# Two later attentions of a transformer chain on one core: the bound on the squared norms is taken by GpSimd, right in front of its power, and the sums of squares alternate between two places

## The reference

```python
def l2norm(t):
    return t / jnp.clip(jnp.linalg.norm(t, axis=-1, keepdims=True), 1e-12)
...
h = shift_token(x)
qkv = h @ wqkv
q, k, v = jnp.split(qkv, 3, axis=-1)
q, k, v = (to_heads(q), to_heads(k), to_heads(v))
q = l2norm(q) * qs
k = l2norm(k) * ksc
q, k = rotary_xpos(q, k)
o = local_attention(q, k, v)      # windows of 128, each with the one before
x = x + o @ wo
```

## Time and profile before

| | before |
|---|---|
| median of 3 runs | 1781.7 us (1779.3 to 1782.6) |
| the profiled execution | 1780.4 us, its span 1778.7 |
| TensorE matmuls busy | 1709.4 us, 96% of the span |
| VectorE busy | 1544.5 us, 87% |
| ScalarE busy | 1164.5 us, 65% |
| GpSimd busy | 1046.2 us, 59% |
| TensorE's granted clock, whole span | 0.993 |

### The profile page before, as it was taken

One profiled execution on the slowest core, in us unless ns is written; L12 is line 12 of the kernel. 1 busy time (PEld: TensorE's weight loads), 2 busy tenths in 40 slices (PEclk: granted clock), 3 DMA queues, 4 the chain that ended last, 5 costly groups with the idle time before them and its releaser, 6 DMA issues.

```text
span 1778.7 us, 43290 instructions
## 1 busy us (share of the span) xinstructions
PE 1709.4 (96%) x15168; PEld 1464.3 (82%) x15168; DVE 1544.5 (87%) x3863; ACT 1164.5 (65%) x3024; POOL 1046.2 (59%) x996
## 2 busy tenths in 40 slices
PE   6999999999999899999998999989999999999997
PEld 4787777789998788888887888868888888878886
DVE  7888888868878899999997677789999999967776
ACT  6999988854445687877775434357777777743332
POOL 3676566534434677777673455367778777634343
PEclk9999999999999999999999999999999999999999
DMA  3111211032322222222223434332222222141221
GB/s 107 38 38 38 72 40 32 26 107 79 108 69 76 84 65 80 62 78 77 64 68 95 144 105 127 100 105 72 71 69 77 65 78 73 50 117 54 82 83 36
DMA packets 183075, 133.83 MB, mean 75 GB/s; under 512 B 21080, under 2 KB 182112, under 8 KB 182112
## 3 DMA queue, kind: packets, MB, share of 16 engines
q1 hardware_dynamic: 182880, 131.37, 24.4%
HBM read 92.52 MB, written 38.80 MB: 74 GB/s over the span
## 4 chain that ended last, share of the span: by engine, by line
PE 63%; DVE 13%; ACT 13%; issue 7%; DMA 2%; SPq 1%; POOL 0%; DVEq 0%; ACTq 0%; POOLq 0%
PE psum L601 14%; PE psum L603 14%; PE psum L602 14%; ACT b_probs L1864 5%; PE psum L716 3%; PE psum L698 3%; PE psum L937 3%; DVE masked L1361 3%; PE psum L905 3%; PE psum L918 2%; ACT a_probs L1745 2%; PE psum L879 2%; PE psum L651 1%; DVE a_neg_max L1229 1%; DVE psum L1227 1%
## 5 line engine op out<-in xcount | busy, mean ns | idle before, releaser
L1864 ACT ACTIVATE b_probs<-masked,neg_max 128x256 f32<-128x256 f32 (+1 forms) x512 | 249.9, 490 | 133.1 <-DVE neg_max L1361 133.1
L601 PE MATMUL psum<-wa_hi,b_h_hi 128*128 128x512 f32 (+1 forms) x576 | 234.7, 407 | 5.0 <-DVE wa_lo L1156 3.4
L603 PE MATMUL psum<-wa_hi,b_h_lo 128*128 128x512 f32 (+1 forms) x576 | 215.8, 375 | 0.0
L602 PE MATMUL psum<-wa_lo,b_h_hi 128*128 128x512 f32 (+1 forms) x576 | 214.9, 373 | 0.0
L601 PE MATMUL psum<-g_h_hi,wm_hi 128*128 128x512 f32 (+1 forms) x480 | 190.8, 397 | 3.5 <-POOL g_h_lo L2129 2.4
L2089 POOL TENSOR_TENSOR g_in<-g_in,minus_half 128x16 f32<-128x16 f32 x64 | 187.8, 2935 | 4.5 <-DVE g_in L1313 4.5
L603 PE MATMUL psum<-g_h_hi,wm_lo 128*128 128x512 f32 (+1 forms) x480 | 189.4, 395 | 0.0
L602 PE MATMUL psum<-g_h_lo,wm_hi 128*128 128x512 f32 (+1 forms) x480 | 189.2, 394 | 0.0
L1361 DVE CUSTOM_DVE_ANT_0 masked<-psum,mask 128x256 f32<-128x256 f32 (+1 forms) x512 | 176.6, 407 | 7.1 <-PE psum L905 7.0
L1483 POOL TENSOR_TENSOR g_in<-g_z,g_in 128x512 f32<-128x512 f32 x62 | 80.3, 1296 | 162.8 <-DVE g_in L1307 157.7
L601 PE MATMUL psum<-wm_hi,u_hi 128*128 128x256 f32 x576 | 164.0, 285 | 0.1
(11 more groups left out here) (168 smaller groups left out, 5533.7 us busy)
## 6 DMA issues: line engine op xcount, KB each, us to landing
b_inv_t<-inverse_rows SPq DMA_DIRECT2D x128, 128.0 KB, 3.1
x_mid<-y_out SPq DMA_DIRECT2D x96, 128.0 KB, 2.3
rope_in<-in_rope SPq DMA_DIRECT2D x64, 128.0 KB, 2.3
x_res<-x_state SPq DMA_DIRECT2D x64, 128.0 KB, 2.8
g_in<-x_mid SPq DMA_DIRECT2D x32, 256.0 KB, 3.8
g_old<-x_state SPq DMA_DIRECT2D x16, 512.0 KB, 4.1
out_x<-g_fin SPq DMA_DIRECT2D x15, 512.0 KB, 2.9
w_raw<-in_w_mlp_b SPq DMA_DIRECT2D x2, 2154.0 KB, 8.8
```

The source lines that it names most:

```text
L601: nc.tensor.matmul(out, a_hi, b_hi, start=first, stop=False)
L602: nc.tensor.matmul(out, a_hi, b_lo, start=False, stop=False)
L603: return nc.tensor.matmul(out, a_lo, b_hi, start=False, stop=last)
L1864: ins = nc.scalar.activation(out, src, ACT.Exp, bias=neg_max[:, r, k:k + 1], scale=-1.0, accum_out=row_sum[:, n % 2, 4 * r + k:4 * r + k + 1])
```

## The change

GpSimd now takes the maximum with 1e-24 itself, as a new instruction directly in front of its power, with the constant in the instruction; VectorE's L1313 and the tile `least` are gone. The sums of squares go to one of two places by the parity of the block, and VectorE waits before it writes a place until the power of two blocks ago is done. `rotate_q` gets a wait for VectorE's own sums, which read the squares that it overwrites.

```diff
--- before.py
+++ after.py
@@ -186,7 +186,6 @@
         ident = sbuf("ident", [P, P])
         zero_row = sbuf("zero_row", [P, 2, P])
         minus_half = sbuf("minus_half", [P, 16])
-        least = sbuf("least", [P, 16])
         b_inv = sbuf("b_inv", [P, 32])
         b_inv_turned = sbuf("b_inv_turned", [P, 32])
         vec_a = sbuf("vec_a", [P, 16])
@@ -245,7 +244,8 @@
         g_in_flat = [t[:].rearrange("p c a d -> p (c a d)") for t in g_in]
         cos_part = [g_in_flat[0][:, 512 * i:512 * i + 512] for i in range(2)]
         rope = g_in_flat[0][:, 1024:1280].rearrange("p (a d) -> p a d", a=4)
-        norm2, norm2c, rnorm = [g_in_flat[0][:, 1280 + 16 * i:1296 + 16 * i] for i in range(3)]
+        norm2 = [g_in_flat[0][:, 1280 + 16 * i:1296 + 16 * i] for i in range(2)]
+        norm2c, rnorm = [g_in_flat[0][:, 1312 + 16 * i:1328 + 16 * i] for i in range(2)]
         rot = [g_in_flat[1][:, 512 * i:512 * i + 512] for i in range(2)]
         b_ctx.close()
 
@@ -1304,16 +1304,14 @@
             def norms(n, i):
 
                 v.wait_ge(S[["q_squared", "k_squared"][i]], g0 + n + 1)
-                nc.vector.tensor_reduce(norm2[:, 8 * i:8 * i + 8], heads(squares[i][:, n % 2, :]), AX.X,
+                if g0 + n > 1:
+                    v.wait_ge(S["rnorm_ready"], g0 + n - 1)
+                nc.vector.tensor_reduce(norm2[n % 2][:, 8 * i:8 * i + 8], heads(squares[i][:, n % 2, :]), AX.X,
                                         ALU.add).then_inc(S["norm2_part"], 1)
-                if i == 0:
-                    v.wait_ge(S["norm2_part"], 2 * (g0 + n) + 2)
-                    if g0 + n > 0:
-                        v.wait_ge(S["rnorm_ready"], g0 + n)
-                    nc.vector.tensor_tensor(norm2c[:], norm2[:], least[:], ALU.max).then_inc(S["norm2_ready"], 1)
 
             def rotate_q(n):
                 v.wait_ge(S["rope_ready"], g0 + n + 1)
+                v.wait_ge(S["norm2_part"], 2 * (g0 + n) + 2)
                 rotate(nc.vector, 0, n, S["q_parts"])
                 v.wait_ge(S["q_parts"], 4 * (g0 + n) + 3)
                 nc.vector.tensor_tensor(cos_part[0][:], cos_part[0][:], squares[0][:, n % 2, :], ALU.add).then_inc(S["q_parts"], 1)
@@ -1670,7 +1668,6 @@
         def _(v):
             nc.vector.memset(zero_row[:], 0.0)
             nc.vector.memset(big[:], -MASKED)
-            nc.vector.memset(least[:], 1e-24)
             nc.vector.memset(b_inv[:], 1.0)
             nc.vector.memset(minus_half[:], -0.5).then_inc(consts_set, 1)
             dve_attention_a(v)
@@ -2085,6 +2082,8 @@
             def inverse_norms(n):
                 if g0 + n > 0:
                     pool.wait_ge(S["k_rot"], g0 + n)
+                pool.wait_ge(S["norm2_part"], 2 * (g0 + n) + 2)
+                nc.gpsimd.tensor_scalar_max(norm2c[:], norm2[n % 2][:], 1e-24).then_inc(S["norm2_ready"], 1)
                 pool.wait_ge(S["norm2_ready"], g0 + n + 1)
                 nc.gpsimd.tensor_tensor(rnorm[:], norm2c[:], minus_half[:], ALU.pow).then_inc(S["rnorm_ready"], 1)
```

## The result

The changed kernel takes 1787.7 us (median of 6 executions, 1785.5 to 1789.2), the kernel before beside it 1780.9 (1779.3 to 1782.6): 1.0036 times as long, 95% interval 1.0026 to 1.0047. Taken again later, beside other executions of before, it was 1787.3, 1.0036 [1.0023, 1.0049]. Forecast were 1778.3 and a range up to 1783.5, so it is slower where I had a small gain, and outside the range. The profiled execution took 1786.4 us, its span 1784.7.

What follows compares the result with a forecast made beforehand. The chain through VectorE's maxima and ScalarE's exponentials was taken to set the pace, TensorE right behind. Plain steps -5.7, split steps +2.8, opening -0.5 gave -3.4 us: 1778.3 for the median, range 1772.5 to 1783.5.

Steps and rivals of the forecast that it cites:

- Plain steps: Later two attentions, steps without a weight split on GpSimd: 12.35 us each, 0.15 shorter, 38 x 0.15 = 5.7 us saved.
- Rival 2: Another wait, on ScalarE or TensorE, takes the max's place at once in plain steps; 1783.2 us at most; chance 0.17.
- Split steps: Steps with GpSimd's weight split ahead of the power: 14 x 0.20 = 2.8 us lost; S is a step's scores' start (L905).
- d: Delay of GpSimd's power by the new maximum and its self-wait: 0.24 us, with ends 0.15 and 1.24.
- rival 3: GpSimd's max is dear, delaying the power before L2072 and L1336: 1783.9 us, or 1798 with a 1.16 start; chance 0.11.
- The two that "escape": Two of 16 split steps, behind a block's short first step where the power has more room, counted as losing nothing.
- The opening: Second layer's opening: L1566, directly behind L1313, can come sooner; 0.5 us saved, bounds 0 and 0.7; first layer 0.
- The memset less: One memset fewer in the changed kernel, counted as worth nothing.

Runs made afterwards that it cites:

- before again: The kernel before, unchanged, run and profiled a second and a third time: 1781.4 us (12 executions) and 1779.5 us (one).

## Why the prediction was wrong

**Plain steps: right.** Forecast -0.15 x 38, measured -0.19 x 38 = -7.2 (36 of them among the 27 steps of each layer, -6.8), the upper bound that I gave; a little of it comes from the addresses. The idle time in front of the maxima is 0.60 us, not 0.8. Rival 2 is out: nothing else took the place of the wait.

**Split steps: here it failed.** I wrote that "a split step grows by d - 0.04 = 0.20 us", with the power ending at S + 6.89 and the tables starting at S + 6.85. The power ended at S + 7.32, they start at S + 7.30, and the step grew by 0.61. The size of d was off too (0.33 to 0.35 for my 0.24), but that would have given 0.30, inside the range. What failed is that I let the power keep its length: the hold added 0.28 us to it, and the 14 split steps cost 8.5 us where I had 2.8. I had read the mutual hold of VectorE and GpSimd as something that befalls VectorE, because L1313 shows it that way nearly 64 times; whichever is issued second waits. The rows were there. The rotation at 759.53 stood 0.20 us behind the power at 759.33, while my own two terms moved the rotation forward by 0.19 and the power back by 0.24. And the trace of before has three powers that are held, two of them at the openings, by the very rotation in question; GpSimd and VectorE:

```profile
550.88 3.29 POOL L2089 TENSOR_TENSOR g_in<-g_in,minus_half 128x16 f32<-128x16 f32 x1 [4.36 <-DVE g_in L1313]
```
```profile
550.73 0.68 DVE L1483 TENSOR_TENSOR g_in<-g_h,g_in 128x512 f32<-128x512 f32 x1
```

From the crossing on, while the power starts inside the rotation's first instruction, its end hangs on that instruction's end and no longer on d. So rival 3, whose price was d x 14, had the right place and the wrong mechanism: my forecast of it turned slower only from a maximum of 0.67 us, and 0.26 did it. None of the three signs that I had named for being wrong came up (plain steps above 12.3 us, split steps shorter, a maximum over 0.4 us), since none of them looked at the power.

**The two that "escape": wrong.** They did not: the short first step grew by 0.3 and the one behind it by 0.9 to 1.1 in each layer, +2.6 together. In the short first step of before the power starts at S + 2.44 and the rotation at S + 2.89; in after the rotation comes first, at S + 2.62, and the power at S + 2.80 takes 3.30 us. GpSimd so enters the next step 0.46 us later than before (its first low half at S + 1.22 instead of S + 0.76), and there the room of 0.45 us that the power had ahead of the rotation is gone. In the second layer it is the maximum that is held in this step, 0.74 us long, and the power behind it keeps its 2.93.

**The opening: right, with a neighbour left out.** Forecast -0.5 for the second layer, measured -0.67 (from the mark at 1147 us to the first step's start, in both profiles of after; 0.0 in the two of before again). The first step of each layer lost another 0.57, which I had not counted. L1313 stood there between the sum of squares and the low halves of the keys (L1340), for which TensorE waits before the next scores; VectorE in before:

```profile
577.50 0.53 DVE L1313 TENSOR_TENSOR g_in<-g_in,least 128x16 f32<-128x16 f32 x1
577.95 0.68 DVE L1340 TENSOR_TENSOR k_t_lo<-psum,k_t_hi 128x512 fp32r<-128x512 f32 x1
```

The low halves start at S + 12.10 there and at S + 11.54 in after, and the next step comes as much sooner.

**What I had left out: the addresses.** "The memset less: nothing" is as forecast, but the tile less moved all that lies behind it by 64 bytes. That cost 2.1 to 2.8 us in the first attention and the first MLP, 1.9 of them in the MLP.

By the runs' numbers the sum is -6.8 (36 plain steps) + 8.5 (14 split) + 2.6 (the two, with the short ones) - 0.8 (the ends) - 1.1 (the first steps) - 0.7 (the opening) + 2.5 (addresses) = +4.2. Measured are +6.2: 1787.5, the median of the 12 executions of after, less 1781.3, that of 84 of before. Some 0.4 of the other 2.0 are in the second layer's second step; where the rest is stays open. The start and each layer's second step vary by 3 to 4 us from profile to profile of one kernel, and a single execution spreads by 1.4 to 1.7 (standard deviation), so two profiles of after don't place them.

## What to carry to other kernels

Where two engines exclude each other, compare the start times of both instructions after the change, not only their durations before it: an order that holds by 0.2 us can turn at once, and then a small delay brings a hold on top of it (here an instruction of 0.26 us made steps 0.61 us longer). A transfer of work between engines and the order of the work around it have to be tried together; here each alone lost 3 and 6 us and both together won 9. Before a loss ahead of the first changed instruction is explained, take a second profile of both kernels, and if a tile went away, put an empty one in its place.

## What was not expected of the hardware

- VectorE's maximum over 128x16 is held by GpSimd's addition with a constant operand as with a tile: 926 and 941 ns in the mean, 174 when free.
- GpSimd's maximum over 128x16 takes 0.24 to 0.26 us, the power 2.91 to 2.94; starting 0.35 us into a VectorE instruction of 0.76 us with two SBUF inputs makes the power 3.19, starting 0.22 into one of 0.82 makes it 3.38; with 0.15 us of the VectorE instruction left it is 2.94.
- Matmuls of 128x256 start each 121.6 ns instead of 116.9 when the tiles that they read lie 64 bytes lower, and a plain step of the changed attentions is 12.160 instead of 12.187 us; what in the address decides was not tried.
